# One summed instruction for the query's parts, a new hand-kept order of steps, and more unread products on TensorE

## The reference, cut to what matters

```python
x = L0_attn_a_x                                    # 8 samples x 512 tokens x 256
x = x + causal_attention(layernorm(x))             # 16 heads of 16, rotary positions
x = x + gated_attention(layernorm(x))              # the 256 tokens of highest gate, 16 heads of 16
x = x + biased_attention(layernorm(x))             # 16 heads of 64, bias by distance
x = x + gated_attention(layernorm(x))              # the same weights as the second layer
```

## Time and profile before

| | |
|---|---|
| median of 3 runs | 2094.7 us |
| the profiled execution | 2098.75 us, of which 2097.0 us are its span |
| PE busy | 1993.4 us (95%) |
| DVE busy | 1541.3 us (73%) |
| ACT busy | 1162.7 us (55%) |
| POOL busy | 696.6 us (33%) |
| instructions | 41715 |

### The profile page before, as it was taken

One profiled execution on the slowest core, in us unless ns is written; L12 is line 12 of the kernel. 1 busy time (PEld: TensorE's weight loads), 2 busy tenths in 40 slices (PEclk: granted clock), 3 DMA queues, 4 the chain that ended last, 5 costly groups with the idle time before them and its releaser, 6 DMA issues.

```text
span 2097.0 us, 41715 instructions
## 1 busy us (share of the span) xinstructions
PE 1993.4 (95%) x15834; PEld 1275.1 (61%) x15834; DVE 1541.3 (73%) x4835; ACT 1162.7 (55%) x2610; POOL 696.6 (33%) x879
## 2 busy tenths in 40 slices
PE   7889999999999999999999999999999999999998
PEld 4476666655666556665566655665556655665666
DVE  8787663877868778678777697786876877867446
ACT  1525664656637565374754646456563756627742
POOL 6212332343412534133422344233342343413320
PEclk8689999999999999999999999999999999999999
DMA  3000121121101211111011210111110121102100
GB/s 143 2 1 9 59 93 43 59 71 34 61 16 49 83 34 44 34 64 58 27 44 47 75 41 27 37 58 64 41 52 11 59 71 34 61 16 69 68 1 21
DMA packets 29062, 98.76 MB, mean 47 GB/s; under 512 B 2880, under 2 KB 11200, under 8 KB 28736
## 3 DMA queue, kind: packets, MB, share of 16 engines
q1 hardware_dynamic: 28864, 96.09, 13.8%
HBM read 91.89 MB, written 4.19 MB: 46 GB/s over the span
## 4 chain that ended last, share of the span: by engine, by line
PE 74%; DVE 16%; ACT 7%; issue 2%; POOL 0%; DMA 0%; SPq 0%; DVEq 0%; POOLq 0%
PE ps L938 20%; PE ps L1657 10%; PE ps L1435 9%; PE ps L1675 9%; PE ps L1665 9%; DVE ps L1290 4%; DVE probs L1381 3%; PE ps L1533 3%; PE ps L1519 3%; ACT PTc L1161 3%; PE ps L1612 3%; PE ps L1624 2%; PE ps L1495 2%; PE ps L1590 2%; ACT PTf L1168 1%
## 5 line engine op out<-in xcount | busy, mean ns | idle before, releaser
L1097 POOL TENSOR_SCALAR probs<-probs,rtotal 128x512 f32<-128x512 f32 x512 | 354.1, 712 | 513.1 <-DVE rtotal L1390 512.8
L1188 ACT ACTIVATE probs<-probs,peak 128x512 f32<-128x512 f32 x512 | 365.1, 714 | 171.9 <-DVE peak L1386 171.0
L1381 DVE CUSTOM_DVE_ANT_0 probs<-ps,band 128x512 f32<-128x512 f32 x512 | 332.7, 687 | 69.7 <-PE ps L1657 69.1
L1197 ACT ACTIVATE PT<-ps 128x512 f32<-128x512 f32 x512 | 262.9, 612 | 42.9 <-PE ps L1665 42.6
L1665 PEld LDWEIGHTS ps<-ident,probs 128*128 128x128 f32 x2048 | 225.2, 141 | 41.7 <-issue 24.1
L1290 DVE CUSTOM_DVE_ANT_0 ps<-ps,later 128x512 f32<-128x512 f32 (+3 forms) x512 | 232.9, 528 | 22.5 <-PE ps L1495 22.0
L1665 PE MATMUL ps<-ident,probs 128*128 128x128 f32 x2048 | 249.1, 275 | 0.1
L1657 PE MATMUL ps<-KT,QT 64*128 64x512 f32 x1024 | 247.5, 616 | 0.0
L1675 PE MATMUL ps<-PT,Vb 128*64 128x512 f32 x1024 | 239.4, 601 | 0.0
L938 PE MATMUL ps<-xnT,wb 128*128 128x512 f32 x512 | 235.2, 605 | 0.6 <-ACT xnT L1122 0.6
L1161 ACT ACTIVATE PTc<-ps 128x384 f32<-128x384 f32 (+1 forms) x384 | 168.3, 544 | 52.9 <-PE ps L1519 51.8
(11 more groups left out here) (156 smaller groups left out, 3352.1 us busy)
## 6 DMA issues: line engine op xcount, KB each, us to landing
band<-in_band SPq DMA_DIRECT2D x64, 896.0 KB, 4.5
wb<-in_w_b SPq DMA_DIRECT2D x64, 384.0 KB, 3.0
x<-in_x SPq DMA_DIRECT2D x16, 256.0 KB, 2.9
out<-x SPq DMA_DIRECT2D x16, 256.0 KB, 2.2
wob<-in_wo_b SPq DMA_DIRECT2D x1, 1024.0 KB, 8.8
wqk<-in_wqk_a SPq DMA_DIRECT2D x1, 512.0 KB, 5.8
cos_t<-in_cos SPq DMA_DIRECT2D x1, 256.0 KB, 5.5
sin_t<-in_sin SPq DMA_DIRECT2D x1, 256.0 KB, 6.2
```

Of the source, the lines that this page charges most:

```text
L1097: last = g.tensor_scalar(unit, unit, rtotal[:, r % 8, e:e + 1], 1.0, ALU.mult, ALU.mult)
L1188: last = a.activation(unit, unit, ACT.Exp, bias=peak[:, r % 8, e:e + 1], accum_out=total[:, r % 8, e:e + 1])
L1197: a.activation(PT[:, k % 2, e, :, tile_of(q)], bank(now, name).rearrange("p (k n) -> p k n", k=NT), ACT.Copy).then_inc(act_read, 1)
L1381: v.tensor_tensor_reduce(out=probs[:, r % ROWS_HELD, e, :], in0=bank(now, name), in1=band[:, k % 2, e, lo:lo + T], scale=1.0, scalar=-3e38 ...
```

## The change

Four things change.

1. `c_rq`, `f_rq`, `c_xq` and `f_xq` are one instruction of 128x1024 where they were two of 128x512; `WORK` has their new durations.
2. The account in `in_order` knows that an operation of DVE marked `dve2` and one of POOL exclude each other also when POOL's comes later in the order: the `dve2` operations that were entered after it are put off.
3. `spare` is now the wait from when the first of the step's banks is free (and PE is) until all can start, and names that bank. The unread products come behind a wait for that bank alone, no longer for all banks, and so also before the many-bank steps `c_p1`, `c_p2`, `f_p1`, `f_p2`. The limits and counts differ: at both ends 8 x (wait - 0.2) where the wait is over 0.4, else 5 x wait where it is over 1.
4. `PLACE` has new numbers, so the order is another one.

```diff
-    "f_rq": [("act", 0.65), ("act", 0.65)],
-    "f_xq": [("dve2", 0.66), ("dve2", 0.66)],
+    "f_rq": [("act", 1.17)],
+    "f_xq": [("dve2", 1.25)],
...
 PLACE = {
-    ("cycle", "b_ln"): [-15576],
...
-        needed, could = t, free["pe"]
...
             if opens:
+                first = []
                 for name, _, banks in units:
...
-                    could = max(could, *empty[at:at + banks])
+                    first.append((max(empty[at:at + banks]), len(first), name))
...
-                spare[x] = needed - could
+                spare[x] = t - max(free["pe"], min(first)[0]), min(first)[2]
...
                 other = taken["pool" if name == "dve2" else "dve2"]
-                t = next((b for a, b in reversed(other) if a <= t < b), t)
-                taken[name] = taken[name][-23:] + [(t, t + us)]
+                t = next((b for a, b, _ in reversed(other) if a <= t < b), t)
+                late = [a for a, _, _ in other if a >= t] if name == "pool" else []
+                if late and late[0] < t + us:
+                    by = t + us - late[0]
+                    for y in dict.fromkeys(y for a, _, y in other if a >= t):
+                        if y in done:
+                            done[y] += by
+                    taken["dve2"] = [(a + by, b + by, y) if a >= t else (a, b, y) for a, b, y in other]
+                    free["dve"] += by
+                taken[name] = taken[name][-23:] + [(t, t + us, x)]
...
+        def pair_of(m, now):
+
+            if now.kind[0] == "c":
+                return [some[:, now.n].rearrange("p e n -> p (e n)") for some in (m.Dq, m.X)]
+            return [some.rearrange("p e c n -> p (e c n)") for some in (m.Dq, m.X)]
...
                         if kind == "f_rq":
                             act.wait_ge(dve_read, plan.unit(Step("f_q", s, l), now))
-                            for e in range(2):
-                                last = a.activation(m.X[:, e], m.Dq[:, e], ACT.Copy, scale=sides[:, 0:1])
-                            last.then_inc(signed_done, 1)
+                            both, parts = pair_of(m, now)
+                            a.activation(parts, both, ACT.Copy, scale=sides[:, 0:1]).then_inc(signed_done, 1)
...
                             dve.wait_ge(signed_done, plan.after("signed", Step(kind[0] + "_rq", s, l, n), now))
-                            for e in range(2):
-                                both, parts = (m.Dq[:, n, e], m.X[:, n, e]) if kind == "c_xq" else (m.Dq[:, e], m.X[:, e])
-                                last = v.scalar_tensor_tensor(out=parts, in0=both, scalar=sides[:, 1:2], in1=parts,
-                                                              op0=ALU.mult, op1=ALU.add)
-                            last.then_inc(halves_q_done, 1)
+                            both, parts = pair_of(m, now)
+                            v.scalar_tensor_tensor(out=parts, in0=both, scalar=sides[:, 1:2], in1=parts, op0=ALU.mult,
+                                                   op1=ALU.add).then_inc(halves_q_done, 1)
...
+                        wait, name = plan.spare.get(now, (0, "o"))
                         ends = stage(now)[0] in ("first0", "first1", "last1")
-                        least = 0.3 if ends else 1
-                        if kind != "c_xt" and plan.spare.get(now, 0) > least:
-
-                            for name in names(now):
-                                room(now, name)
-                            for i in range(int((8 if ends else 5) * plan.spare[now])):
-                                te.transpose(bank(now, names(now)[0])[:, tile_of(i % NT)], ident[:], ident[:])
+                        if kind != "c_xt" and wait > (0.4 if ends else 1):
+
+                            room(now, name)
+                            for i in range(int(8 * (wait - 0.2) if ends else 5 * wait)):
+                                te.transpose(bank(now, name)[:, tile_of(i % NT)], ident[:], ident[:])
```

More of the change, by code:

```diff
@@ L208 @@
[L208 to L214, removed]
@@ new lines @@
+    ("cycle", "f_k"): [2803],
+    ("cycle", "f_ln"): [-26583],
+    ("cycle", "f_m"): [2974, 3174],
+    ("cycle", "f_o"): [3364],
+    ("cycle", "f_p1"): [2909, 2146, 2968, 2936],
+    ("cycle", "f_p2"): [3157, 3207, 2714, 2145],
+    ("cycle", "f_part"): [2341],
+    ("cycle", "f_q"): [2876],
+    ("cycle", "f_rank"): [2715],
+    ("cycle", "f_row"): [2637],
+    ("cycle", "f_rq"): [2714],
+    ("cycle", "f_spread"): [3210],
+    ("cycle", "f_v"): [2878],
+    ("cycle", "f_va"): [3304, 3314],
@@ new lines @@
+    ("cycle", "f_vb"): [2818, 1878],
+    ("cycle", "f_xq"): [2888],
+    ("cycle", "f_y"): [3420, -26301],
+    ("cycle3", "f_gate"): [6360],
+    ("cycle3", "f_gather"): [6449],
+    ("cycle3", "f_hk"): [5867],
+    ("cycle3", "f_hm"): [6300, 6916],
+    ("cycle3", "f_k"): [6624],
+    ("cycle3", "f_ln"): [5519],
+    ("cycle3", "f_m"): [6911, 6955],
+    ("cycle3", "f_o"): [7115],
+    ("cycle3", "f_p1"): [6841, 6842, 6893, 6912],
+    ("cycle3", "f_p2"): [6915, 7004, 6752, 6788],
+    ("cycle3", "f_part"): [3988],
@@ new lines @@
+    ("first0", "f_p2"): [1941, 9074, 10136, 9959],
+    ("first0", "f_part"): [8357],
+    ("first0", "f_q"): [5263],
+    ("first0", "f_rank"): [7410],
+    ("first0", "f_row"): [7477],
+    ("first0", "f_rq"): [5962],
+    ("first0", "f_spread"): [7708],
+    ("first0", "f_v"): [5263],
+    ("first0", "f_va"): [10265, 11111],
+    ("first0", "f_vb"): [3629, 10697],
+    ("first0", "f_xq"): [9110],
+    ("first0", "f_y"): [13937, 6011],
+    ("first1", "c_dk"): [4316, 5277],
+    ("first1", "c_dq"): [4221, 4756],
@@ new lines @@
+    ("first1", "f_p1"): [11531, 10068, 10185, 10988],
+    ("first1", "f_p2"): [13098, 13167, 9529, -4311],
+    ("first1", "f_part"): [-5449],
+    ("first1", "f_q"): [4900],
+    ("first1", "f_rank"): [2075],
+    ("first1", "f_row"): [-1837],
+    ("first1", "f_rq"): [2754],
+    ("first1", "f_spread"): [3086],
+    ("first1", "f_v"): [9972],
+    ("first1", "f_va"): [13842, 14146],
+    ("first1", "f_vb"): [14111, 3733],
+    ("first1", "f_xq"): [7904],
+    ("first1", "f_y"): [23009, 3949],
@@ new lines @@
+    ("last2", "f_ln"): [276],
+    ("last2", "f_m"): [24690, 17948],
+    ("last2", "f_o"): [40188],
+    ("last2", "f_p1"): [22411, 21874, 22810, 13174],
+    ("last2", "f_p2"): [33639, 33859, 19978, -101],
+    ("last2", "f_part"): [-1336],
+    ("last2", "f_q"): [7126],
+    ("last2", "f_rank"): [12713],
+    ("last2", "f_row"): [3461],
+    ("last2", "f_rq"): [-206],
+    ("last2", "f_spread"): [-1336],
+    ("last2", "f_v"): [22357],
+    ("last2", "f_va"): [34799, 36468],
+    ("last2", "f_vb"): [33541, -9706],
@@ L426 @@
+    ("last2", "f_xq"): [17254],
+    ("last2", "f_y"): [41009, 15379],
 }
```

387 lines of the change are left out of this document (163 added, 224 removed).

## The result

The changed kernel takes 2064.1 us, the median of 4 runs (2061.5 to 2064.51), against 2094.6 for the kernel before on the same chip (4 runs): a ratio of 0.985, 95% interval 0.9833 to 0.9867, so it is faster by 1.5%. The forecast was 2065.0. Its profiled execution took 2064.3 us, of which 2062.3 are the span.

A forecast was written before the change was run, and what follows sets the result against it. PE, 95% busy, was taken as limited by 104 us idle, largely DVE and POOL holding each other up, and 1.2 GHz stretches. 12.7 + 6.5 + 9 + 1.5 = 29.7; 2098.75 - 29.7 - 4.05 = 2065.0 us; 2050 to 2087 holds eight in ten.

The forecast's parts named there:

- the distance of that execution from the median: Profiled execution of the kernel before lay 4.05 us over the median of its runs; carried over into the forecast.
- f_part ahead of f_row: Seven layers, samples 1 to 7: POOL's xn_lo misses DVE's comparisons, f_rank's wait falls from 1.31 to 0.2 us; 7.7 us.
- Rival (b): f_part's layers: xn_lo collides with tie operations or the gate's sums, f_rank waits as before; 2074 us, chance 0.10.
- One sum: Last gated layer: DVE through sooner, Vx wait 1.55 to 0.35 us, 7.2 us; waits for gX and X halve, 2.0 us.
- What comes back: PE's next waits for DVE or ACT take back a quarter of 16.9 us, leaving 12.7 us net.
- Clock in the cycles: Six cycles: five of nine stretches at 1.2 GHz go, at 1.3 us each; 6.5 us.
- The beginning: Start to about 150 us: 200 more unread products raise the clock, first scores wait less; 9 us.
- the point of 156: Sign for the beginning: the point reached at 156 us before is reached at 147 us.
- Rival (d): Beginning: clock does not rise and unread products stand in front of needed ones; slower, 2109 us, chance 0.08.
- The end: From 2039.3 us: sample 6's last output step fills a wait and the sum is one; 1.5 us of 9.4 idle.
- (a): Cycles: DVE or ACT takes over behind shortened waits, half to all comes back, dips too; 2078 us, chance 0.15.
- (c): Cycles: the long sum blocks POOL's LO, f_p1 and c_p1 wait for it, costing 7 us; 2077 us, chance 0.09.

The follow-up runs named there:

- e5: Changed kernel with f_part put back behind b_tr in the cycle, no unread products added for it: 2074.0 us, ratio 0.9896.
- e1: Kernel before with only the four pairs of sum instructions made one of 128x1024 each, old order and old unread products: 2086.4 us, ratio 0.9959.
- e2: Changed kernel with the sums as two instructions of 128x512 again, its order and unread products kept: 2074.0 us, ratio 0.9901.
- e6: Changed kernel with POOL's order changed in the cycle, two b_nrm normalisings ahead of f_gather and one behind gLO: 2058.4 us, ratio 0.9822.
- e3: Kernel before with only the new rule for unread products, its order and two-instruction sums kept: 2080.9 us, ratio 0.9931.
- e4: Changed kernel with the old rule for unread products, its order and one sum kept: 2079.9 us, ratio 0.9929.
- e7: Changed kernel without the 30 unread products in front of c_p2 in the cycles: 2070.0 us, ratio 0.9877.
- e10: Kernel before with only DVE's negation of the maximum removed, two-instruction sums, order and unread products kept: 2081.5 us, ratio 0.9926.

## Why the prediction was right, and where it was not

*The total.* The profiled execution before took 2098.75 us, the one after 2064.3: 34.4 less. The forecast took 29.7 off by its terms and 4.05 as the distance of that execution from the median, 33.75 in all. That distance is mostly clock. The profiled execution had a mean of 0.976; of the 29 runs of the kernel before in the three lots, those at 0.976 and 0.977 took 2097.5 to 2100.6 us and those at 0.982 and 0.983 took 2090.6 to 2093.6. So the time came out right with terms that are short by about what the double count gave: the distance is itself dips of the clock, which I had entered as a term of its own. That 2065.0 lies within 1 us of the measured time is luck to that extent: two misses of 4 to 5 us cancel. By stretches of the two traces, the beginning gave 14.8 us for the 9 forecast, the six cycles 19.7 for 12.7 + 6.5, the end 0.3 for 1.5. Of my own signs one failed: f_p1's wait for Vx was to be under 0.5 us and is 1.26.

*f_part ahead of f_row*, 7.7 us. Right in mechanism, short in size: in all seven layers f_rank's wait went altogether (I had left 0.2), and e5 gives 9.9 us for this move in the six of the cycles alone, of which 7.9 are the wait; the rest is small waits that went with it. The PT copies and the Vb behind the roundings cost nothing that shows, as assumed. Rival (b) is out.

*One sum*, 7.2 + 2.0 us. The sum of the two was about right, 8.0 and 9.9 by e1 and e2, dips included, and the division wrong. The step that failed is "POOL's gLO ends where it ended, so that DVE is through at about 897.1, 1.2 us sooner; the 1.55 us wait falls to 0.35". The sum did end sooner, but gLO's time has to pass somewhere: the negation, DVE's next instruction on SBUF alone, was held until gLO ended, and the wait fell to 1.26, 1.7 us in six cycles. What I had booked as 2.0 us, the waits for gX and X, brought the larger part, with the maxima behind them and three dips fewer in e1; that the sum of the two terms fits is luck. The Trainium skill, SBUF — State Buffer, section "SBUF: two separate sides", would have told: the pair goes to whoever starts first, for its whole instruction, and a DVE operation in a 2-port mode takes part. The trace agrees if the negation of 128x2 is such an operation: 1.07 us for 0.17. I had looked for two-input operations only, though the comparisons of the earlier trace rows, which were stretched too, are not such.

*What comes back*, 4.2 us. By size near (f_p1's first wait grew from 0.4 us, for gX, to 1.00, for LO, 3.6 us in six cycles), by cause not: it was neither DVE nor ACT as the next bound but POOL, on which `b_nrm` came directly ahead of gLO and DVE's long sum then held gLO up. That POOL's lateness is the part that has to go e6 shows. I had gone by the order of ACT, DVE and PE alone.

*Clock in the cycles*, 6.5 us. Under-sized: eight of nine dips went, not five. The link to single waits did not hold either. In the cycles there are nine before, six in e1, five in e3, e4 and e7, and one after and in e2; e5 has f_rank's wait of 1.31 us back and still only one. So four of the eight hang on the 30 unread products in front of c_p2 (e7, 5.9 us). The sum of idle time does not explain the others: e10 is idle in its cycles for about as long as the changed kernel, some 43 us, and has nine dips, while e5 with 51.6 us has one. What the kernels with at most one dip share is the new order together with those 30 products. What decides one dip stays open.

*The beginning*, 9 us. Right in mechanism, under-sized: the lead at the biased layer of sample 0 (192.4 us before) is 12.7 us, and 14.8 at that of sample 1. Ten to eleven of them are the unread products (e3, e4), one to four the order, one to two the sum. The clock was 0.93 and 1.00 there for 0.65 and 0.68. The step that was reached at 151.5 is reached at 139.0, so the point of 156 lies near 143.5, not 147. Of the 11.5 us that DVE was idle from 26 to 104 us, 8.8 went into the lead where I had taken 6, and 2.6 follow up to 150 where I had taken 1.5. Rival (d) is out.

*The end*, 1.5 us: 0.3. PE's idle time there fell by 2.4 us, but sample 6's output step, which was to fill a wait, stood in front of f_gather, where about 2 us of the lead were lost; the last f_rank waited 0.3 us longer.

*Rivals (a) and (c).* Little of (a) showed: cycles of 247.8 us. Of (c) two pieces are real. One is in every cycle: gLO of the first gated layer takes 3.5 us for 2.6 beside the long sum, and f_p1 waits 1.00 us for it (6.0 us in the six cycles, where the wait for gX had taken 2.4). So the mechanism of (c) is there, at 3.6 us net for the 7 that I gave it, but the gain of the sum that (c) gave up came all the same. The other: the first sum of the program ran at 24.92, and POOL's instruction beside it took 2.24 us where the like one took 1.26 in peace, with PE idle for LO for 2.7 us. It has a price of 1 us, once.

## What to carry to other kernels

When two engines hold each other up at a port, follow the holder's whole duration down the victim's queue: making the struck instruction one does not remove the hold, it passes to the next instruction that uses the port, however small. Here, folding 256 negations of two columns into the reduce brought 15 us on either kernel, more than the sum (8 to 10), with a few arguments and one wait changed; how much of that is the hold and how much the shorter way to ACT, no run parts. And where two engines meet, a lead of 0.3 us can decide which of them is held (e10). And products that nothing reads were worth 13 to 16 us on a kernel whose PE was 95% busy, most of it in the stretch where another engine was the bound.

## What the runs showed of the hardware

The time of one and the same kernel follows its mean granted clock closely: the kernel before ranged from 2100.6 us at 0.977 to 2090.6 at 0.982, while the changed kernel, at 0.997 or 0.998, took 2061.5 to 2064.5. The spread looks narrower too (3 us), but over 4 runs on one chip against 29 on three; the 4 runs of the kernel before beside it spread over 2.1 us, so that is not shown. A dip of 3.4 us to 1.2 GHz cost about 1.4 us here (e7: 249.3 us for a cycle with one, 247.9 without).

Dips can be regular: in e7 all five in the cycles came at the same place of a cycle, 249.2 us apart, and the clock was down while PE worked without a gap; what it had done before was to wait 1.3 us for c_p2's maxima in each cycle.

Unread transposes kept the clock at 2.4 GHz for whole stretches (1.00 from 26 to 104 us in e3, for 0.65 and 0.68 in the kernel before with the same order), in which the old rule with fewer of them left it at 0.74 to 0.77 on average (e4). That is against the Trainium skill, TensorE: Matmul & The Clock Gate, "Part 4: PE-mode transpose", by which they do not count as activity in the same way. The profile lists these transposes of a float32 identity as MATMUL.

A DVE operation of 128x2 elements took 1.07 to 1.12 us when it met POOL's pair of subtractions in the last gated layer (changed kernel and e1), and ended within 0.1 us of that pair's end. Its median over 256 is 0.17 us; 34 of the 256 in the changed kernel, and 19 in the kernel before, took over 0.3. The hold goes both ways: beside DVE's sum of 1.48 us POOL's pair took 3.5 us for 2.5.
